# Two attention and feed-forward layers on one core: projection tiles in one group, scores and values in alternation

## The reference, cut to what matters

```
x = x + tanh(g_xattn[0]) * xattn0(layernorm(x), ctx)
x = x + tanh(g_ffn[0])   * ffn0(layernorm(x))           # relu
x = x + tanh(g_xattn[1]) * xattn1(ctx, layernorm(x), mask)
x = x + tanh(g_ffn[1])   * ffn1(layernorm(x))           # rounded, piecewise linear gelu

def xattn(query, value):                                 # 16 heads of 32
    q = query @ wq + bq;  k = value @ wk + bk;  v = value @ wv + bv
    attn = softmax(q k^T / sqrt(32))                     # over 154 keys
    return (attn v) @ wd + bd
```

## Time and profile before

| | before |
|---|---|
| median of 3 runs (lowest to highest) | 2675.35 us (2675.24 to 2675.56) |
| profiled execution | 2679.4 us |
| its span, first to last instruction | 2677.5 us |
| mean granted TensorE clock | 0.966 |
| PE busy | 2487.4 us (93%) |
| DVE busy | 1461.5 us (55%) |
| ACT busy | 1075.8 us (40%) |
| POOL busy | 508.8 us (19%) |

### The profile page before, as it was taken

One profiled execution on the slowest core, in us unless ns is written; L12 is line 12 of the kernel. 1 busy time (PEld: TensorE's weight loads), 2 busy tenths in 40 slices (PEclk: granted clock), 3 DMA queues, 4 the chain that ended last, 5 costly groups with the idle time before them and its releaser, 6 DMA issues.

```text
span 2677.5 us, 32104 instructions
## 1 busy us (share of the span) xinstructions
PE 2487.4 (93%) x12864; PEld 1854.4 (69%) x12864; DVE 1461.5 (55%) x2222; ACT 1075.8 (40%) x1734; POOL 508.8 (19%) x407
## 2 busy tenths in 40 slices
PE   3899999999999999997479999999889999999997
PEld 3557666688888888885355666665667778778776
DVE  4456556432222222221655555554688889888887
ACT  3243443432222222221323333334465666656664
POOL 1011211350000000001101111111652222222221
PEclk8799999999999999998689999999899999999999
DMA  3001211421100110001310111121401010101000
GB/s 132 32 16 64 80 48 64 146 79 48 47 16 32 47 48 16 32 32 68 103 44 29 61 61 60 61 76 54 155 25 39 28 36 32 48 17 48 32 23 26
DMA packets 87940, 140.91 MB, mean 53 GB/s; under 512 B 4848, under 2 KB 27760, under 8 KB 87792
## 3 DMA queue, kind: packets, MB, share of 16 engines
q1 hardware_dynamic: 87792, 138.87, 15.3%
HBM read 105.30 MB, written 33.55 MB: 52 GB/s over the span
## 4 chain that ended last, share of the span: by engine, by line
PE 37%; DVE 9%; ACT 2%; issue 2%; DMA 1%; POOL 0%; ACTq 0%; DVEq 0%
PE l_lay_bank L66 16%; PE l_lay_score L66 10%; DVE l_at_at_grid L978 2%; DVE l_at_at_next L974 1%; DVE l_at_full L969 1%; PE l_lay_score L1204 1%; PE l_lay_values L1265 1%; PE l_lay_score L1206 1%; PE l_lay_score L1246 1%; PE l_lay_score L1252 1%; PE l_lay_sums L1277 1%; PE l_lay_values L1269 1%; DVE l_at_h_lo L984 1%; PE l_lay_bank L1160 1%; DVE l_at_xTf_lo L875 1%
## 5 line engine op out<-in xcount | busy, mean ns | idle before, releaser
L66 PE MATMUL l_lay_score<-l_at_tw_hi,l_at_h_hi 128*128 128x512 f32 x1024 | 409.3, 400 | 28.1 <-DVE l_at_h_lo L984 28.1
L66 PE MATMUL l_lay_score<-l_at_tw_hi,l_at_h_lo 128*128 128x512 f32 x1024 | 404.9, 395 | 0.0
L66 PE MATMUL l_lay_score<-l_at_tw_lo,l_at_h_hi 128*128 128x512 f32 x1024 | 404.3, 395 | 0.0
L66 PE MATMUL l_lay_bank<-l_at_xTf_hi,l_at_tw_hi 128*128 128x512 f32 x1024 | 403.9, 394 | 0.0
L66 PE MATMUL l_lay_bank<-l_at_xTf_lo,l_at_tw_hi 128*128 128x512 f32 x1024 | 402.4, 393 | 0.0
L66 PE MATMUL l_lay_bank<-l_at_xTf_hi,l_at_tw_lo 128*128 128x512 f32 x1024 | 402.3, 393 | 0.0
L954 DVE TENSOR_TENSOR l_at_h_lo<-l_at_full,l_at_h_hi 128x512 fp32r<-128x512 f32 x128 | 97.8, 765 | 492.7 <-ACT l_at_h_hi L727 492.7
L580 POOL TENSOR_TENSOR l_at_at_next<-l_at_at_next,l_at_at_grid 128x512 f32<-128x512 f32 x128 | 186.5, 1457 | 514.8 <-ACT l_at_at_next L743 514.8
L722 ACT ACTIVATE l_at_full<-l_lay_bank,l_lay_b 128x512 f32<-128x512 f32 x128 | 88.2, 689 | 477.3 <-PE l_lay_bank L66 477.3
L66 PEld LDWEIGHTS l_lay_score<-l_at_tw_hi,l_at_h_hi 128*128 128x128 f32 x1024 | 193.4, 189 | 80.8 <-DVE l_at_h_lo L984 37.9
L66 PEld LDWEIGHTS l_lay_score<-l_at_tw_hi,l_at_h_lo 128*128 128x128 f32 x1024 | 193.4, 189 | 45.5
(11 more groups left out here) (186 smaller groups left out, 4241.4 us busy)
## 6 DMA issues: line engine op xcount, KB each, us to landing
stream<-l_at_xg SPq DMA_DIRECT2D x24, 1024.0 KB, 4.3
l_at_x_in<-stream SPq DMA_DIRECT2D x24, 1024.0 KB, 5.6
l_at_xg<-stream SPq DMA_DIRECT2D x24, 1024.0 KB, 5.6
l_at_tw_raw<-in_l_w SPq DMA_DIRECT2D x64, 256.0 KB, 5.4
l_at_x_in<-in_x SPq DMA_DIRECT2D x8, 1024.0 KB, 6.6
l_at_xg<-in_x SPq DMA_DIRECT2D x8, 1024.0 KB, 5.5
out<-l_at_xg SPq DMA_DIRECT2D x8, 1024.0 KB, 4.3
l_at_maskT_in<-in_maskT SPq DMA_DIRECT2D x8, 512.0 KB, 4.4
```

Of the source, the lines that this page charges most:

```text
L66: done = nc.tensor.matmul(out, lhs[a], rhs[b], start=first and n == 0, stop=last and n == len(passes) - 1)
```

## The change

It touches PE, ACT and DVE. Tiles 1, 2 and 3 of the next chunk's projection are made in one group between s0 and s1, in both layers on PE, and ACT's evictions of them in the plain layer follow it. In the plain layer v2 comes directly behind s3, ahead of r01; and r23 comes behind the first two maxima instead of ahead of them, with DVE's `c_back` for tiles 2 and 3 behind its first two maxima. In the plain layer's last chunk, which has no maxima, r23 follows r01 directly. The norm layer keeps the rest of its order.

```diff
 @block.scalar
                 if not norm:
                     if more:
-                        q_front(it + 1, (1,))
+                        q_front(it + 1, (1, 2, 3))
                     else:
                         relu_hi(1)
                 exps_main(it, 1)
                 c_evict(it, 0)
-                if more and not norm:
-                    q_front(it + 1, (2, 3))
                 exps_main(it, 2)
                 c_evict(it, 1)
                 exps_main(it, 3)
+                if not norm:
+                    c_evict(it, 2)
                 if it:
                     cT_back(it - 1, (0, 1))
-                if more and norm:
-                    q_front_norm(it + 1, (0, 1))
-                c_evict(it, 2)
+                if norm:
+                    if more:
+                        q_front_norm(it + 1, (0, 1))
+                    c_evict(it, 2)
                 if it:
                     cT_back(it - 1, (2, 3))
                 c_evict(it, 3)
 @block.vector
-                if it:
+                if it and norm:
                     c_back(it - 1, (2, 3))
                 for m in range(NM):
                     max_of(it + 1, m)
+                    if m == 1 and it and not norm:
+                        c_back(it - 1, (2, 3))
                     if m == 1 and norm:
                         qT_front(it + 1, (2, 3))
 @block.tensor
                 scores_main(it, 0)
                 if more:
-                    q_front(it + 1, (1,))
+                    q_front(it + 1, (1, 2, 3))
                 else:
                     first_product(1)
                 scores_main(it, 1)
                 values_of(it, 0)
-                if more:
-                    q_front(it + 1, (2, 3))
                 scores_main(it, 2)
                 values_of(it, 1)
                 scores_main(it, 3)
+                if not norm:
+                    values_of(it, 2)
                 if it:
                     recips(it - 1, (0, 1))
-                if more and norm:
-                    qT_front(it + 1, (0, 1))
-                values_of(it, 2)
-                if it:
+                if norm:
+                    if more:
+                        qT_front(it + 1, (0, 1))
+                    values_of(it, 2)
+                if it and (norm or not more):
                     recips(it - 1, (2, 3))
                 if more:
                     for m in range(NM):
                         max_of(it + 1, m)
                         if m == 1:
+                            if it and not norm:
+                                recips(it - 1, (2, 3))
                             values_of(it, 3)
```

## The result

| | kernel before | changed kernel |
|---|---|---|
| median, runs beside each other | 2675.56 us (5 runs) | 2688.09 us (5 runs) |
| ratio, 95% interval | 1 | 1.0045, [1.0031, 1.0058] |
| again, beside later runs | 2677.39 us (16 runs) | 2686.82 us (6 runs) |
| ratio, 95% interval | 1 | 1.0036, [1.0024, 1.0048] |
| profiled execution, its span | 2679.4 us, 2677.5 us | 2688.1 us, 2686.2 us |

The changed kernel is slower, by 12.5 us in the first comparison and by 9.4 us in the second. The forecast was +10.4 us and 2685.7 us.

What follows compares the result with a forecast made beforehand. PE, busy 52.74 of 52.8 us in a plain chunk, was taken to bound the kernel. Terms 10.0 + 1.3 - 0.2 - 0.7 = +10.4 us, applied to the 2675.35 us median, gave 2685.7 us; range 2679 to 2697 us.

Steps and rivals of the forecast that it cites:

- (d): Plain chunks 1 to 6: output projection's first product (y0) waits for DVE's low parts of the context; +1.67 us per chunk.
- (a): PE, projection tiles 1 to 3 in one group: one pair of tile-shape switches fewer, -0.20 us per plain chunk.
- (b): PE, plain layer: v2 directly behind s3, ahead of both reciprocal transposes, saves 0.18 us.
- (c): PE, r23 behind the first two maxima: PE stands 0.1 to 0.2 us for its POOL copies.
- (e): Plain chunk 7, no maxima behind it: y0 starts at about 506.66 instead of 505.39, +1.3 us.
- (f): Chunk 0 gains only the merged group, -0.2 us; norm layer gains 0.10 us in each of seven chunks, -0.7 us.
- all six waits with the clock down and at their bound: Plain chunks 1 to 6, upper range end: half-clock after every wait, first DVE pair at 3.36 us; given as 2697 us.
- The clock did not fall: Rival: PE's clock falls after each new wait, 1.6 us lost per event, 2695.3 us in all; chance 0.12.
- the other side: Rival: context's low parts come before PE reaches y0, so the savings stand alone, 3.4 us, 2672.0 us; chance 0.12.
- The exponentials did not bind: Rival at s2: ACT's exponentials come late behind v0 alone; half the chunks at 1 us each give 2693 us; chance 0.03.

Runs made afterwards that it cites:

- the first experiment: Kernel before with only projection tiles 1 to 3 put in one group; 2676.18 us against 2677.18 us, ratio 0.9995.
- the experiment with three maxima: Changed kernel with three maxima instead of two ahead of DVE's products for tiles 2 and 3; 2706.46 us, ratio to before 1.0105.

## Why the prediction was right

**The late y0, step (d), carries the result.** From the start of r01 to the end of the last low part the prediction had 0.70 + 2.60 + 1.46 + 2.68 = 7.44 us. Measured in chunk 4: 0.70 + 2.59 + 1.42 + 2.66 = 7.37 us (353.05, 353.75, 356.34, 357.76, 360.42). y0 started 7.43 us after r01 where 7.49 us were forecast (the release took 0.06 us; the 0.05 us in the forecast had no row behind them), and the first matmul took 0.33 us to the next, the 0.10 us over the pitch that the prediction added. A chunk was +1.60 us instead of +1.67 us; the difference is within rounding the 0.06 us here and the 0.03 us that (a) gave more. That the first pair would go in 2.60 us and not in 3.36 us, once ACT was free, was right too: DVE has no gap between the products and the low parts.

**(a)** -0.20 us forecast for the merged group; -0.23 us in the first experiment. **(b)** v2 to r01 to maxima came as worked out (350.34, 353.05, 353.90, which is 2.71 and 0.85 us).

**(c)** had its size right and its place in the sum wrong. From r01 to v3 PE took 2.69 us, where (d) has 0.85 + 1.60 = 2.45 us. The kernel with r23 late alone, whose copies are ready in time, shows the parts: maxima 0.67 us and r23 0.97 us to v3, 1.64 us together for the 1.60 us of the forecast. In the changed kernel r23 takes 355.74 - 354.58 = 1.16 us, 0.19 us more, and that is the standing for POOL's copies that (c) put at 0.1 to 0.2 us and (d) left out of PE's stretch. The rows are those of the kernel with r23 late alone, then the weight loads (PEld) of r23's second half in the changed kernel:

```profile
350.84 0.83 PE L1208 MATMUL l_lay_score<-l_at_k_bd,l_at_qT_hi 128*128 128x308 f32 x4
351.51 1.03 PE L1313 MATMUL l_lay_bank<-ident,l_at_r_wide 128*128 128x128 f32 x8
352.48 1.06 PE L1267 MATMUL l_lay_values<-l_at_p_tail,l_at_v_tail 128*32 128x512 f32 x8
```

```profile
355.15 0.42 PEld L1314 LDWEIGHTS l_lay_bank<-ident,l_at_r_wide 128*128 128x128 f32 x4 [0.18 <-POOL l_at_r_wide L566]
```

So PE reached y0's turn 5.79 us after r01 and not 5.55 us, and the wait from start to start was 1.64 us where 1.89 us were forecast. It changes nothing in the chunk, since y0 started when DVE's chain was done.

**(e)** Chunk 7: y0 is at 516.63, against 505.39 11.24 us later, where y0 of chunk 6 was 9.82 us later (469.21 against 459.39). That is +1.42 us for the forecast +1.3 us, and 0.10 us of it is chunk 6's first matmul. The chain took 6.01 us from r01 (510.62) to y0; 6.03 us were forecast. The transposes r23 there wait 0.43 us for POOL's copies, which the prediction did not name:

```profile
512.15 1.23 PE L1314 MATMUL l_lay_bank<-ident,l_at_r_wide 128*128 128x128 f32 x8 [0.43 <-POOL l_at_r_wide L566]
...
516.63 0.50 PE L66 MATMUL l_lay_bank<-l_at_wd_hi,l_at_xT_hi 128*128 128x512 f32 x1 [0.55 <-DVE l_at_xT_lo L937]
```

It cost nothing, since y0 waited behind it.

**(f)** In chunk 0 the stretch from s0 to s3 went from 18.45 to 18.27 us, -0.18 us. In the norm layer five chunks, from one wait for the maxima to the same one five chunks on, took 1831.12 - 1502.18 = 328.94 us after and 1819.24 - 1489.86 = 329.38 us before, -0.09 us each; the 0.10 us was the middle between two bounds and had no row behind it, so that it came this close is luck.

**Sum.** 6 x 1.60 + 1.42 - 0.18 - 7 x 0.09 = +10.2 us, against +10.4 us forecast, and +12.5 and +9.4 us in the medians. Two ends of the prediction's ranges do not follow from its own terms: 1.5 us under 2685.7 us is 2684.2 us and not 2683 us, and all six waits with the clock down and at their bound make 2685.7 + 9.6 + 5.4 = 2700.7 us and not 2697 us. The measured times lie well inside either way.

The two profiled executions differ by 8.7 us only. In the last attention chunk of the norm layer, that of the kernel before took 3.0 us longer, at a lower clock. The same matmuls in two stretches, before and then after:

```profile
1885.52:1904.41 18.89, 14.37 (x64) 11.61 (x65) 8.42 (x13) 6.51 (x11) 8.96 (x6) 0.89 0.70 222
1904.41:1926.22 21.81, 19.52 (x72) 15.55 (x73) 9.66 (x11) 7.28 (x12) 13.13 (x11) 0.86 0.44 145
```

```profile
1897.35:1914.44 17.09, 13.07 (x64) 10.55 (x64) 8.41 (x13) 6.51 (x11) 8.96 (x6) 1.00 0.74 247
1914.44:1935.06 20.62, 18.32 (x72) 14.61 (x72) 9.66 (x11) 7.27 (x12) 13.16 (x11) 0.91 0.45 152
```

The first stretch begins in both behind a wait of 1.7 us (1.72 and 1.69 us), the second behind one of 3.46 and of 2.97 us; they are 1.80 and 1.19 us apart. No instruction differs there between the two kernels, so this is not the change's. Without it the two would be 11.7 us apart; 0.52 us of that lies ahead of s0 of chunk 0 (119.04 and 119.56), and the rest over the sum was not traced.

**The rivals.** The clock did not fall: 1.00 in chunks 1 to 6 behind waits of 1.48 us, as behind the 1.79 us of the earlier trace rows. The Trainium skill says, on its page "TensorE: Matmul & The Clock Gate", Part 1, that TensorE at rest goes back to the half rate; the experiment with three maxima agrees at 3.48 us, five times of six, and the changed kernel's waits of 1.48 us do not show it. Twelve waits without a fall don't make 1.48 us safe, as the last section shows. DVE's being in time (the other side) would have needed a chain under PE's own stretch, 5.79 us as measured, and fell with the first y0. The exponentials did not bind: in the first experiment PE is busy for 52.50 of 52.56 us with s2 right behind v0.

## What to carry to other kernels

When PE is full, moving its own work about is worth a tenth of a microsecond per switch saved, and each switch must be set against what the moved instruction starts elsewhere. Here transposes of 0.85 us in all, moved back by 2.7 us, started a chain of 7.4 us on DVE that had 1.3 us of slack. Before moving an instruction on the engine that is busy, follow what it releases through every engine to the next instruction that PE needs, and compare that chain with PE's own stretch. The same holds for moving it forward: r01 5 us earlier bought nothing until ACT's order was changed along with it.

## What was not expected of the hardware

The same wait does not always cost the clock. In one execution, five waits of 3.48 us were followed by half clock for some 3 us and one of the same length, in the same loop, by none, 1.5 us apart in the length of the chunk. Shorter waits do it too. In the last attention chunk of the norm layer, which no experiment touches, PE waits 1.7 us and 1.05 us, 0.6 us apart, in all twelve profiles (in the kernel before these end at 1885.52 and 1887.20). Over the 5 us behind the first of the two the granted clock is 1.00 in six of them; in the other six, the kernel before among them, it is 0.66 to 0.74. From there to the end of the first wait of the feed-forward part the same matmuls take 36.0 to 40.7 us. What decides it is not shown by any run here. Over 23 executions the kernel before ran from 2674.26 to 2682.37 us, so a comparison of two single profiles of it says nothing under some 8 us, while the length of a chunk repeats within 0.02 us (54.36 and 54.38 us in the changed kernel's two profiles).
